# Perceiver block on one core: the part up to the first key scores in another order

## The reference

```python
x = x + xattn(layernorm(x), ctx, ctx, mask, Wq, bq, Wk, bk, Wv, bv, Wo, bo)   # x (4,128,128), ctx (4,2048,128)
x = x + ssm(layernorm(x), W_in, W_out, Wp, bp, alpha_log, delta_bias, log_gamma)
x = x + ffn(layernorm(x), w1, b1, w2, b2)
# xattn: 16 heads of 8
q = (Q @ Wq.T + bq); k = (K @ Wk.T + bk); v = (V @ Wv.T + bv)                 # split in heads
scores = einsum('bhqd,bhkd->bhqk', q, k) / sqrt(8) + mask
out = (softmax(scores) @ v) @ Wo.T + bo
```

## Time and profile before

| | us |
|---|---|
| median of 3 runs | 290.56 |
| lowest and highest | 287.4, 291.3 |
| profiled execution, device time | 291.72 |
| its span in the trace | 289.9 |
| PE busy in the span | 264.6 (91%) |

### The profile page before, as it was taken

One profiled execution on the slowest core, in us unless ns is written; L12 is line 12 of the kernel. 1 busy time (PEld: TensorE's weight loads), 2 busy tenths in 40 slices (PEclk: granted clock), 3 DMA queues, 4 the chain that ended last, 5 costly groups with the idle time before them and its releaser, 6 DMA issues.

```text
span 289.9 us, 9826 instructions
## 1 busy us (share of the span) xinstructions
PE 264.6 (91%) x3991; PEld 191.7 (66%) x3991; DVE 223.1 (77%) x407; ACT 210.1 (72%) x441; POOL 101.1 (35%) x225
## 2 busy tenths in 40 slices
PE   8699789999999999999999999999999997841975
PEld 7376457676767676676777777777777664631965
DVE  4776878887878999887888898889889941539871
ACT  3575358888788888888888888888887785298032
POOL 5366765634444333333444454411121120100220
PEclk9999869999999999999999999999999999885699
DMA  6896935887532324242333322222222000000001
GB/s 196 293 312 179 290 94 154 241 210 202 165 115 75 119 66 120 77 137 80 118 108 102 119 66 66 67 80 84 70 84 77 2 3 2 1 0 0 0 2 38
DMA packets 21081, 30.55 MB, mean 105 GB/s; under 512 B 4272, under 2 KB 15052, under 8 KB 20908
## 3 DMA queue, kind: packets, MB, share of 16 engines
q1 hardware_dynamic: 17708, 28.00, 31.9%
q0 software_dynamic: 624, 1.06, 1.4%
q10 hardware_dynamic: 2704, 0.85, 1.2%
HBM read 22.43 MB, written 7.47 MB: 103 GB/s over the span
## 4 chain that ended last, share of the span: by engine, by line
PE 81%; DVE 8%; issue 4%; ACT 3%; DMA 2%; POOL 1%; ACTq 0%; POOLq 0%; DVEq 0%
PE ps L494 24%; PE ps L477 15%; PE ps L458 11%; PE ps L587 5%; PE ps L353 4%; PE ps L505 4%; PE ps L548 4%; PE ps L540 3%; PE ps L369 3%; PE ps L347 2%; PE ps L364 2%; DMA x_sb<-in_x_dram 2%; DVE pmax L1305 2%; PE ps L772 1%; ACT probs L877 1%
## 5 line engine op out<-in xcount | busy, mean ns | idle before, releaser
L1305 DVE TENSOR_REDUCE pmax<-ps 128x2 f32<-128x1024 f32 x128 | 156.1, 1224 | 28.8 <-PE ps L458 28.0
L877 ACT ACTIVATE probs<-ps 128x512 f32<-128x512 f32 x256 | 139.0, 595 | 19.9 <-PE ps L477 17.6
L477 PE MATMUL ps<-q_max,k_rows 59*128 59x128 bf16 x1024 | 82.4, 219 | 0.5 <-ACT probs L877 0.2
L494 PE MATMUL ps<-probs,v_all 128*9 128x128 f32 x2048 | 80.8, 276 | 0.7 <-ACT probs L877 0.7
L458 PE MATMUL ps<-k_rows,q_all 56*128 56x512 bf16 x256 | 78.7, 388 | 2.2 <-DVE pmax L1305 2.0
L477 PEld LDWEIGHTS ps<-q_max,k_rows 59*128 59x128 bf16 x1024 | 55.9, 94 | 5.2 <-ACT probs L877 3.1
L494 PEld LDWEIGHTS ps<-probs,v_all 128*9 128x9 f32 x2048 | 43.4, 90 | 14.9 <-ACT probs L877 1.0
L1114 POOL CAST max_cols<-negmax 128x2 bf16<-128x2 f32 x32 | 6.2, 193 | 119.6 <-DVE negmax L1311 119.6
L458 PEld LDWEIGHTS ps<-k_rows,q_all 56*128 56x128 bf16 x256 | 23.2, 94 | 21.3 <-issue 11.3
L347 PE MATMUL ps<-ones 128*128 128x128 f32 x86 | 15.0, 352 | 11.1 <-ACT k_parts L1003 10.1
L347 PEld LDWEIGHTS ps<-ones 128*128 128x128 f32 x86 | 14.5, 265 | 11.5 <-ACT k_parts L1003 10.5
(11 more groups left out here) (186 smaller groups left out, 330.0 us busy)
## 6 DMA issues: line engine op xcount, KB each, us to landing
k_rows<-k_parts_dram SPq DMA_DIRECT2D x59, 192.0 KB
k_parts_dram<-k_parts SPq DMA_DIRECT2D x16, 384.0 KB, 3.7
ctx_buf<-in_ctx_dram SPq DMA_DIRECT2D x16, 256.0 KB, 6.0
k_rows<-k_parts_dram SPq DMA_DIRECT2D x59, 32.0 KB
mask_sb<-in_mask_1x1xSxS_ff_dram SPq DMA_DIRECT2D x1, 1024.0 KB, 8.7
q_all<-q_rows_dram SPq DMA_DIRECT2D x2, 336.0 KB
k_rows<-k_parts_dram POOLq DMA_DIRECT2D x3, 192.0 KB, 3.8
q_rows_dram<-q_parts SPq DMA_DIRECT2D x2, 288.0 KB, 3.7
```

The costliest lines, as they stand in the source:

```text
L477: t = pe.matmul(dst, k_rows[rows, i % 4, at:at + P], q_max[rows, i % 2, :], start=not masked, stop=True, skip_group_check=masked)
L494: t = pe.matmul(ps[at:at + HEAD_COLS, 6, 0:P], v_all[:, KT * (i // PAIRS) + 4 * c + j, first + HEAD_COLS * h: first + HEAD_COLS * h + HEAD ...
L877: act.activation(probs[:, u % CHUNKS, h, :], ps[:, 4 + h, :], ACT.Exp).then_inc(probs_ready, 1)
L1305: dve.tensor_reduce(pmax[:, i % 2, :, c], ps[:, bank:bank + 2, :], AX.X, ALU.max).then_inc(pmax_ready, 1)
```

## The change

- Transfers: ACT's queue now has `x[0]`, Wq and the two biases, and no stores or loads of queries; `ident` goes through POOL's queue ahead of its first memset; `x[1:4]` through SP's behind the mask. SP's queue then has: the three query stores, key chunks 0 and 1, ctx 4 and 5, the load of the query rows, key chunk 2, pair 0's first half, key chunk 3, ctx 6 and 7, pair 0's second half.
- Key products 0 to 3 take banks 4, 5, 6, 7, and no longer wait for `rest_k`; the value products 0 to 3 banks 0, 1, 6, 7, the last two behind `r1_ready` 3 and 4. Weights and queries turn in banks 2 and 3.
- POOL splits the queries of batch 0; DVE makes the third part of key chunks 1 and 3 and POOL those of 0 and 2.
- DVE's memset of `k_rows` is cut in three around the work on `x[0]`; the cast of `ident` goes behind `rest_k(3)`; `normalise_x` of batches 1 to 3 goes behind `max_unit(1)`.
- In `attend` the scores of units 0 to 3 come earlier in the order and `early_v` 6 and 7, `early_k(7)` later; ACT copies the queries' `xnT` one chunk later, and takes the values of chunk 7 behind `exp_unit(0)`. One warm-up product less.

```diff
-    WARM_UP = 7
+    WARM_UP = 6
@@ sync
             sp.dma_start(mask_sb[:, :], mask.rearrange("a b q k -> (a b q) k")).then_inc(ld["mask"], 16)
-            for n in range(EARLY, CTX_SLOTS):
-                load_ctx(n)
+            sp.dma_start(x_sb[:, 1:B, :], x[1:B].rearrange("b t d -> t b d")).then_inc(ld["x_rest"], 16)
...
-            store_chunk(0)
-            for n in range(CTX_SLOTS, FIRST):
-                load_ctx(n)
-            for n in range(1, EARLY):
-                store_chunk(n)
-            sp.wait_ge(once("k_ones_ready"), 1)
-            for half in range(2):
+            def load_first_head(half):
                 for c in range(2 * half, 2 * half + 2):
                     sp.wait_ge(k_first[c], 16)
                 load_half_pair(sp, 0, 0, slice(KEYS // 2 * half, KEYS // 2 * half + KEYS // 2), first_heads[half])
+
+            for part in range(PARTS):
+                if part < 2:
+                    sp.wait_ge(once("q_step"), 2 * part + 2)
+                else:
+                    sp.wait_ge(once("q_parts_ready"), 1)
+                store_q(sp, part, first_tokens)
+            store_chunk(0)
+            store_chunk(1)
+            for n in range(EARLY, CTX_SLOTS):
+                load_ctx(n)
+            sp.wait_ge(once("q_stored"), 16 * 3)
+            sp.wait_ge(once("q_all_zeroed"), 1)
+            load_q(sp, first_tokens, once("q_loaded"))
+            store_chunk(2)
+            sp.wait_ge(once("k_ones_ready"), 4)
+            load_first_head(0)
+            store_chunk(3)
+            for n in range(CTX_SLOTS, FIRST):
+                load_ctx(n)
+            load_first_head(1)
@@ tensor, up to the branch
-            turn(ps[:, 2, 0:P], w_kv[:, 0, :])
+            turn(ps[:, 2, 0:P], w_kv[:, 0, :]).then_inc(once("kqv_turned"), 1)
+            turn_ctx(1, 1)
             pe.wait_ge(ld["vec_qk"], 32)
-            pe.transpose(ps[:, 2, 3 * P:3 * P + 2], vec_nat[0:2, :], ident[0:2, 0:2]).then_inc(once("kqv_turned"), 1)
-            turn_ctx(1, 1)
-            pe.wait_ge(once("kT_ready"), 1)
+            pe.transpose(ps[:, 3, 3 * P:3 * P + 2], vec_nat[0:2, :], ident[0:2, 0:2])
+            pe.wait_ge(ld["wq"], 16)
+            turn(ps[:, 3, P:2 * P], w_kv[:, 2, :]).then_inc(once("kqv_turned"), 1)
+            pe.wait_ge(once("kT_ready"), 2)
             project_k(4, 0)
...
             turn_ctx(1, 3)
-            pe.wait_ge(r1_ready, 1)
-            project_k(4, 2)
+            project_k(6, 2)
             pe.wait_ge(ld["wv"], 16)
-            turn(ps[:, 3, P:2 * P], w_kv[:, 1, :]).then_inc(once("kqv_turned"), 1)
-            pe.wait_ge(r1_ready, 2)
-            project_k(5, 3)
+            turn(ps[:, 2, P:2 * P], w_kv[:, 1, :]).then_inc(once("kqv_turned"), 1)
+            project_k(7, 3)
             pe.wait_ge(once("qT_ready"), 3)
-            project_v(6, 0)
-            project_v(7, 1)
+            project_v(0, 0)
+            project_v(1, 1)
             pe.wait_ge(r1_ready, 3)
+            project_v(6, 2)
+            pe.wait_ge(r1_ready, 4)
+            project_v(7, 3)
             turn_ctx(4, 4)
...
             def attend(masked):
+                scores(0, masked)
+                scores(1, masked)
                 early_k(5)
                 early_turn(6)
-                scores(0, masked)
-                scores(1, masked)
                 early_v(5)
                 pe.wait_ge(v_ready, 3)
                 pe.wait_ge(once("xn_ready"), B)
                 turn_xn(6, 1, B - 1)
+                scores(2, masked)
                 early_k(6)
+                scores(3, masked)
                 early_turn(7)
-                scores(2, masked)
-                early_v(6)
-                scores(3, masked)
-                early_k(7)
...
-                early_v(7)
+                early_v(6)
                 scores(4, masked)
+                early_k(7)
                 pe.wait_ge(once("out_bank_zeroed"), 1)
                 turn_max(0).then_inc(turned, 1)
...
                 keyscores(0, 1, masked)
+                early_v(7)
                 scores(6, masked)
@@ gpsimd
+            gp.dma_start(ident[:, :], ident_in).then_inc(ld["ident"], 16)
             gp.memset(ones[:, :], 1.0).then_inc(once("ones_ready"), 1)
...
+                    gp.tensor_copy(q_parts[:, part, tok], src[:, tok]).then_inc(once("q_step"), 1)
...
-            for n in range(EARLY):
+            for n in range(0, EARLY, 2):
                 third(n)
@@ vector
+                if n % 2:
+                    dve.wait_ge(k2_ready, n + 1)
+                    dve.tensor_tensor(k_parts[:, 2, keys], k_r1[:, 1, :], k_parts[:, 1, keys], ALU.subtract
+                                      ).then_inc(once("k3_odd_ready"), 1)
...
+            fill_rows(slice(0, 2))
             dve.wait_ge(ld["x"], 16)
             moments((0,))
+            fill_rows(slice(2, 3))
             normalise_x((0,), 0)
+            fill_rows(slice(3, 4))
+            split_q_first(3, first_tokens, 0)
+            for n in range(EARLY):
+                rest_k(n)
             dve.wait_ge(ld["ident"], 16)
             dve.tensor_copy(ident_bf[:, :], ident[:, :]).then_inc(once("ident_bf_ready"), 1)
-            rest_k(0)
-            split_q_first(2, first_tokens, 0)
-            split_q(first_tokens, 0)
-            split_q_rest(first_tokens, 0)
-            for n in range(1, EARLY):
-                rest_k(n)
             mask_magnitude()
...
-            normalise_x((1, 2, 3), 1)
             for u in range(UNITS):
                 max_unit(u)
+                if u == 1:
+                    normalise_x((1, 2, 3), 1)
```

## The result

| | before | after |
|---|---|---|
| median of 20 runs each | 290.39 us | 293.52 us |
| lowest and highest | 287.40, 292.34 | 290.68, 298.90 |
| profiled execution, device time | 291.72 | 291.80 |
| its span in the trace | 289.9 | 290.0 |
| ratio after to before, with its 95% interval | | 1.0087 (1.0064 to 1.0110) |

The changed kernel is slower: by 3.1 us in the medians (1.1%), by 0.9% in the ratio, where 293.1 us was forecast. The ratio leaves out the executions that are over 1.5% longer than the fastest of their kernel (six of after, two of before), and the medians keep them. The profiled execution of after is one of its quicker ones, and that of before one of its slower ones, so the two spans are equal though the medians are not. The traces show the delay, and also what paid it back in this pair.

A forecast was written before the change was run, and what follows sets the result against it. TensorE was taken as the bound, busy 91% of 289.9 us, so the loop's start counts. Branch +1.5, idling +2.3, values 7 −1.0, small gaps −0.3 gave +2.5: 292.4 of span, 293.1 against the median; range 287.5 to 297.

The forecast's parts named there:

- The bounds of the terms: Uncertainties of ident, GpSimd's small steps, ctx landing and second half, put at +1 to +4 us, or 291.5 to 294.5.
- First transfers: Kernel's start: `x[0]` lands at about 4.1 instead of 7.4 us; `ident` by GpSimd's queue, first turn about 4.4 instead of 4.14.
- The splits: Key chunks and queries: VectorE's third part 0.7 us, GpSimd's query steps 1.5, chunk 1 ready at 14.3.
- SP's queue: Ctx chunk 4 issued at 15.0 behind stores, lands at 18.9; TensorE idles 1.7 us; branch at 23.25 instead of 21.79.
- Behind the branch: From the branch to the loop: new idling +2.3 us, `turn_max(0)` at 33.9 instead of 31.42, loop start 38.0 against 35.5.
- The clock in the hole: Rival, 20%: clock falls while TensorE waits for ctx chunk 4, 17.2 to 20.2 us; +1 to +2 more, 294.8 us.
- the full clock at the loop: Rival, 15%: the loop starts at full instead of about half clock, saving some 2.6 us; with 1 us delay, 289.
- the dip at the loop: About half clock in before from 34 to nearly 41 us; without it 5.4 us of work cost some 2.6 less.
- it decides once the delay is under 2.6 us: Condition of the faster rival: full clock at the loop outweighs the loop start's delay only if that is under 2.6 us.

The follow-up runs named there:

- the two kernels of the last part: Before with value product 7 moved behind the first keyscores: 0.9958, 289.29 us; before with six unread products of ones in the waits ahead of the loop: 0.9952, 289.28 us.
- an edit that lies 10 us behind it: After, with ACT's copy of the queries' `xnT` put one chunk earlier again: ratio to before 1.0097, 292.84 us.

## Why the prediction was right, step by step

**The size.** 293.1 forecast, 293.5 measured. What was forecast is a delay of the loop's start of 2.5 us; in the traces it was 3.4. The forecast's sum had no term for the clock (it stood among the rivals), and the clock acted in both directions: it held at the loop's start (1.8 us back in the pair of traces), and the low-clock executions of after lose more than those of before (4.3 us instead of 2.5). In the medians this left +3.1 us of the 3.4. That the missing 0.9 us of delay and the clock nearly cancel is luck, so the closeness of the number says less than the steps do. The bounds of the terms, if all are added, give +0.7 to +5.5 rather than +1 to +4; the delay lies within both.

**First transfers: a term mis-sized.** The first turn was put at 4.4, at most 1 us late; it came at 5.78. `x[0]` came a little earlier than forecast, its statistics start at 3.57. The timelines of VectorE and POOL and the issue to landing of `ident`, in after:

```profile
5.26 1.72 DVE L1198 TENSOR_SCALAR xn<-x_sb,mv,rstd 128x128 f32<-128x128 f32 x1
...
12.83 1.36 DVE L1271 CAST k_parts<-k_r 128x512 bf16<-128x512 f32 x1
14.22 0.69 DVE L1274 TENSOR_TENSOR k_parts<-k_r,k_parts 128x512 bf16<-128x512 f32 x1
...
26.76 0.85 DVE L1198 TENSOR_SCALAR xn<-x_sb,mv,rstd 128x128 f32<-128x128 f32 x3
...
1.25 0.74 POOL L1020 DMA_DIRECT2D ident<-in_ident_dram  x1 [0.80 <-POOLq L1588]
...
4.95 1.95 POOL L1047 MEMSET v_all<- 128x1024 f32 x1
...
11.05 0.29 POOL L1055 CAST q_parts<-q 128x128 bf16<-128x128 f32 x1 [4.15 <-DVE q L1210]
...
12.75 1.15 POOL L1069 TENSOR_TENSOR k_parts<-k_r,k_parts 128x512 bf16<-128x512 f32 x1
```

```profile
ident<-in_ident_dram POOLq DMA_DIRECT2D x1, 64.0 KB, 4.5
```

Two things were too small. The issue of `ident` at 1.25 puts PE's warm-up 1.28 us later (2.27 against 0.99), where 0.6 was taken; by that alone the first turn comes at 4.99, as it does in four of the later traces. And `ident` lands 4.5 us after its issue here; the forecast took the 2.5 to 3.1 us of the earlier trace rows, which were loads of 16 KB issued late. In the seven traces that have this load on POOL's queue it landed after 3.2 to 4.6 us. The Trainium skill ("DMA: Bandwidth & Descriptors", Anatomy of one DMA — SWDGE (gpsimd) path) fits such a load with 2.0 us and the bytes at 436 KB a us, which makes an estimate of 2.15 us for this one. The traces do not agree: none is under 3.2 us. Still, the miss of 1.4 us was mostly taken up by 10 us: the query product came at 10.21, forecast 9.85, 10.77 before.

**The splits: right, by other terms.** VectorE's third part took 0.69 us (0.7 taken), and POOL's query split 1.7 from 11.05 to its third part (1.5 taken). Chunk 1's cast beside POOL's third took 1.36 us (1.05 taken), since POOL's pass began just ahead of it and lasted 1.15. Chunk 1 was ready at 14.9, forecast 14.3. `xn`'s normalisation, 0.35 us in before, took 1.72 beside POOL's memset of `v_all`. Both rows agree with the Trainium skill ("SBUF — State Buffer", Who interferes with whom): the later engine waits for the earlier one's pass to end. So part of the work moved to POOL stayed on VectorE's path, as a wait.

**SP's queue: right.** The forecast's loss starts here. The timeline of SP, then issue to landing:

```profile
13.93 1.54 SPq L233 DMA_DIRECT2D k_parts_dram<-k_parts  x2
15.51 1.41 SPq L270 DMA_DIRECT2D ctx_buf<-in_ctx_dram  x2
```

```profile
ctx_buf<-in_ctx_dram SPq DMA_DIRECT2D x1, 256.0 KB, 3.7
```

Chunk 4's load was issued at 15.51 (15.0 forecast), landed after 3.7 us (3.9), and its turn came at 19.26 (18.9), with 1.35 us of idle ahead of it (1.7). Value product 4 ended at 23.42 and scores 0 came at 24.06; 22.6 and 23.25 were forecast. The last 0.64 us is as forecast. Of the 0.8 us, 0.3 is the load, and 0.5 lies between the turn and the end of value product 4, 4.2 us against 3.7: the sum left out the two small products over the mask's maxima (0.17), and the rest is a tenth of a us in each of four steps.

**Behind the branch: right, 0.5 to 0.8 late throughout.** Forecast and measured: turn_xn's wait 0.7 and 0.70, scores 2 27.8 and 28.28 (a wait of 0.45 us for their rows was forecast, and there was none), the query product's wait 1.15 and 1.07, `turn_max(0)` 33.9 and 34.72, from there to the loop 4.1 and 4.22. Value product 7 hid behind the maxima as put. The timeline ends turn_xn's wait with ACT's copy of the values (`v_all`), but PE waits there for only three copies, long made, and for the normalisation. That is VectorE's row at 26.76, which ends at 27.61, as the forecast had it.

**The chances: two rivals held in part.** The clock in the hole was given 20%, the full clock at the loop 15%, as if each execution had one story. The trace of after shows the second, that of the early copy of `xnT` the first, and the table by clock both. The forecast had one price for the dip at the loop (2.6 us); the pair of traces shows 1.8 and the two kernels of the last part 1.2 to 1.4 of the median. Where it stood as "it decides once the delay is under 2.6 us", the delay alone, 3.4 us, decided it.

**What stays open.** The front costs 0.5% beside the order behind the branch and ctx 4. Its trace has both a slow start (2.4 us at the query product) and new waits behind it (2.6 us). What brings the slow start about in some executions, how often it comes, and how the cost is shared between the two, no run here settles. The parts are not additive either: 0.8 us for the load's place, 1.7 for the order behind the branch, and taking out both left 0.5% of loss, about as much as taking out the first alone.

## What to carry to other kernels

Where one engine sets the end, follow the first instruction of its long loop back, and price every queue that its inputs stand in: moving a load behind a store in a queue written out by hand moves it by the whole chain ahead of that store, here its issue from about 4 to 15.5 us, and mending it alone moved part of the wait to the next load. If the granted clock falls just ahead of such a loop, put work that must be done anyway into that wait; here it was worth 0.4% of the time (0.1 to 0.7), while no reordering of transfers tried here gained anything clear of noise. And compare executions at the same granted clock before reading a difference of spans: the profiled pair here was equal, and the kernels were not.

## What the runs showed that was not expected

- `ident` through POOL's queue was issued at 1.25 us and landed after 3.2 to 4.6 us in seven traces; through ACT's queue it landed after 3.0 to 3.4 in the seven others.
- Three waits in a row on PE (0.73, 1.35 and 0.69 us in after) left its clock as it was: the product at 20.60 took 1.13 us. With an edit that lies 10 us behind it the waits were 0.73, 1.82 and 0.69, and the same product at 20.85 took 2.07.
- At the start of the trace the granted clock reads 1.00 while products take twice their time (2.07 us for the key product at 7.71 with `ident` on ACT's queue, 1.12 for the one at 7.85 in after), so in the first 13 us the clock is read from durations, not from the record.
- Six products that nothing reads, two at a time in 0.71 us, made a kernel of 290 us quicker by 0.5%.
